# Loading the first four expert tiles on a condition of their own, in a conv, attention and mixture-of-experts kernel

## The chip, the cores and the metric

The kernel runs on one core of a Trainium2 chip. Time is the device time of one execution, in microseconds, as the median of several runs. The profile is of one further execution, which has its own time.

## The reference, cut to what matters

The input is 16 images of 256 channels and 14 by 14 points, all in float32. A bottleneck block of three convolutions with batch norms comes first, then linear attention over the 196 points of each image (a token is a point, 3136 in all), then a mixture of experts over all tokens:

```python
t = t + attention(layernorm(t))
flat = layernorm(t)                        # 3136 tokens x 256
probs = softmax(flat @ gate_w + gate_b)    # 8 experts
top_p, top_i = top_k(probs, 2)
top_w = top_p / (sum(top_p) + 1e-9)
for e in range(8):
    h = gelu(flat @ w1[e] + b1[e])         # 256 -> 1024
    y = h @ w2[e] + b2[e]                  # 1024 -> 256
    out += comb[:, e] * y                  # comb holds top_w at top_i, else 0
```

Every token goes to two experts, so the experts together get 6272 rows. The kernel computes an expert only on the rows that chose it.

## The kernel before, in words

**Three stretches.** First the convolutions. Then the attention as a software pipeline over the 16 images, in 25 slots (`SLOTS_A`), with the experts' weights split and stored beside it. Then the experts, as 56 slots (`SLOTS`) of one tile of 128 rows each, in the order of the experts.

**From the router to the experts.** Two images make a group, and there are 8 groups. For each group VectorE finds the two experts of each token (`route_top`), counts, and TensorE ranks the rows within their expert (`route_rank`); VectorE turns the ranks into row numbers (`route_slots`). GpSimd (POOL) then sends the rows to DRAM, to a buffer `norm_rows` (in the rows of the profile `rows_by_expert`) in which each expert has a region of 26 blocks of 128 rows: 8 indirect DMAs of 98 rows per group (`send_rows`, L440), which count on four semaphores `s_rows[g % 4]`, 128 for a group. A row is 265 numbers: 256 normalised values, 8 weights, and the token's number.

**The end of each expert.** The last tile of an expert is seldom full. So, once the counts are known, a block of 128 neutral rows (`padrow`) is written behind the last row of each expert (`pad_ends`, L260 to L265): experts 0 to 3 from the queue of SyncE (SP), 4 to 7 from that of ScalarE (ACT). Each pad is a register load of its address (L264) and a DMA (L265). One more pad, for the block that stands for "no tile", is written near the start of the kernel.

**The tile table.** TensorE sums the counts over the partitions (L812), and VectorE makes the table in 25 small dependent steps, counted by `s_tab` (`tile_table`, L1208 to L1278): for each slot the expert (`tbi[:, 0]`) and the block of `norm_rows` (`tbi[:, 1]`, "the column"), then packed forms of the experts, the end of each expert's run of tiles (`last_tile`), and a mask of experts by slot. The steps are a generator, and so interleaved with the last group's `route_slots`.

**The start of the experts.** ACT's stream at that place is: its four pads; a wait for the whole table; waits for all rows of all groups and for all pads; then `load_rows(0)`, `(1)`, `(2)`; then a loop of slots. Slot `m` of ACT holds, in this order, the copies of tile m-2's turned hidden values (L636), the copy of tile m's turned rows (L625), the gelu of tile m-1 (L630), and `load_rows(m + 3)`. One `load_rows` reads the block's number from the table into a register (L616) and issues a DMA of 128 rows (L619). TensorE waits for the table and then for tile 0's rows, transposes them (L829), and so on: transposes of a tile, then the first product of the tile before (L836), then the second product of the tile before that. VectorE adds biases (L1356, L1362), makes the low halves of the split operands (L1335, L1341), and scales; POOL adds the results to the output. SP, after its pads, reloads weights for experts 2 to 7, each when the last tile of the expert two before has passed.

Of the kernel before, what the change touches and what calls it, by code (L numbers as in the profile page):

```python
# [24 lines left out]
I32 = mybir.dt.int32  # L25
FR = mybir.dt.float32r
U32 = mybir.dt.uint32
ALU = mybir.AluOpType
# [45 lines left out]
RING = 8  # L74
XR, YS = 8, 4


# [6 lines left out]
def moe_block(nc, x, w1t, w2t, w3t, norms, res_scale, wqkv, wout, bout, gate_w, gate_b, ew1, ew2, eb, out):  # L84
# [5 lines left out]
    with ctx:  # L90
# [44 lines left out]

        cnti = sb("cnti", [128, E], I32)
        ntl = sb("ntl", [128, 2, E])
        lt = sb("lt", [128, E, E])
# [35 lines left out]
        with ExitStack() as scope:  # L174
            def mem(name, shape):
                return scope.enter_context(nc.sbuf_tensor(name, shape, F32))
            rows = mem("rows", [HALF, RING, 2, ROW])
            tc = mem("tc", [128, 2, 2, HW])
            xh = mem("xh", [HALF, 2, 2, C])
            qe = mem("qe", [HALF, 2, 2 * C])  # L180
            qn = mem("qn", [HALF, 2, 2 * C])
            ek = mem("ek", [128, 2, 2, HW])
            vT = mem("vT", [128, 3, 2, HW])
            ekt = mem("ekt", [HALF, 2, 2, C])
            cT = mem("cT", [128, 2, 2, 128])
            pr = mem("pr", [128, 2, 2, C])
            xT2 = mem("xT2", [128, 2, 2, HW])
        xr = sb("xr", [128, XR, ROW])
        xrTh = sb("xrTh", [128, 2, C], FR)
# [29 lines left out]
        s_tok = sem("token_numbers_written")  # L219
        s_ends = [sem(f"expert_ends_padded_by_{n}") for n in ("sync", "act")]  # L220
        s_res = sem("residual_written")
# [36 lines left out]


        def pad_ends(eng, which):  # L260

            eng.wait_ge(s_tab, 1)
            for e in range(which * E // 2, (which + 1) * E // 2):
                at = eng.value_load(pad_at[0:1, e:e + 1], min_val=0, max_val=128 * (NONE - 1))  # L264
                eng.dma_start(norm_rows[bass.ds(at, 128), :], padrow[:, :]).then_inc(s_ends[which], 16)  # L265


        @block.sync
        def _(sp):
# [58 lines left out]
            sp.wait_ge(s_const, NCONST)  # L328
            sp.dma_start(norm_rows[128 * NONE:128 * (NONE + 1), :], padrow[:, :]).then_inc(s_padw, 16)
            sp.dma_start(out[TOKENS:TOKENS + 128, :], padrow[:, 0:C]).then_inc(s_padw, 16)  # L330
# [8 lines left out]
            for n in range(SLOTS_A):  # L339
# [11 lines left out]
                if n == UNITS - EARLY + 2:  # L351
                    load_expert(1)
            pad_ends(sp, 0)
            sp.wait_ge(s_tab, TAB_STEPS)
# [6 lines left out]
        def _(pool):  # L361
# [92 lines left out]
            pool.wait_ge(s_res, 16 * B)  # L454
            pool.wait_ge(s_padw, 32)

# [15 lines left out]
        def _(act):  # L472
# [130 lines left out]

            act.activation(rs[:, 2:3], rs[:, 1:2], ACT.Gelu)
            pad_ends(act, 1)
            act.wait_ge(s_tab, TAB_STEPS)
            for a in range(RING // 2):
                act.wait_ge(s_rows[a], 128 * len(range(a, B // 2, RING // 2)))
            act.wait_ge(s_padw, 32)
            for a in range(2):  # L610
                act.wait_ge(s_ends[a], 16 * E // 2)
            blocks = norm_rows.rearrange("(c p) r -> c p r", p=128)

            def load_rows(i, r):
# [42 lines left out]
        def _(pe):  # L657
# [245 lines left out]
        def _(dve):  # L903
# [304 lines left out]
            def tile_table():  # L1208
                dve.wait_ge(s_cntp, 1)
                link(V.tensor_tensor(pad_at[:, :], psV[0:HALF, 0:E], expert_row[:, 0, :], ALU.add))  # L1210
                link(V.tensor_scalar(cnti[:, :], psV[:, 0:E], 127.0, None, ALU.add))
                yield
                dve.wait_ge(s_tab, tab[0])
                link(V.tensor_scalar(cnti[:, :], cnti[:, :], 7, None, ALU.logical_shift_right))
                yield
                dve.wait_ge(s_tab, tab[0])
                link(V.tensor_scalar(ntl[:, 0, :], cnti[:, :], 1.0, None, ALU.max))
# [8 lines left out]
                link(V.tensor_copy(last_tile[:, :], ntl[:, 1, :]))  # L1226
                yield
                dve.wait_ge(s_tab, tab[0])

                link(V.tensor_tensor(big[:, 0], iotf[:, 0:64].unsqueeze(2).to_broadcast([128, 64, E]),  # L1230
                                     ntl[:, 1, :].unsqueeze(1).to_broadcast([128, 64, E]), ALU.is_ge))
# [3 lines left out]
                yield  # L1235
                dve.wait_ge(s_tab, tab[0])
                link(V.tensor_tensor(big[:, 1], big[:, 0], ntl[:, 0, :].unsqueeze(1).to_broadcast([128, 64, E]), ALU.mult))
                yield
                dve.wait_ge(s_tab, tab[0])
                link(V.tensor_reduce(tb[:, 2, :], big[:, 1], X, ALU.add))  # L1240
                yield
                dve.wait_ge(s_tab, tab[0])
                link(V.tensor_tensor(tb[:, 3, :], iotf[:, 0:64], tb[:, 2, :], ALU.subtract))
                yield
                dve.wait_ge(s_tab, tab[0])
                link(V.scalar_tensor_tensor(out=tb[:, 3, :], in0=tb[:, 1, :], scalar=float(COLS), in1=tb[:, 3, :],
                                            op0=ALU.mult, op1=ALU.add))
                yield
                dve.wait_ge(s_tab, tab[0])
                link(V.tensor_scalar(tbi[:, 1, :], tb[:, 3, :], float(NONE), None, ALU.min))  # L1250
                yield
# [4 lines left out]
                link(V.tensor_copy(tbi[:, 0, :], tb[:, 4, :]))  # L1256
                yield
                dve.wait_ge(s_tab, tab[0])

                link(V.tensor_copy(tb[:, 0, 2:SLOTS + 2], tb[:, 4, 0:SLOTS]))  # L1260
# [152 lines left out]
MAGIC = 0x5F3759DF + 1  # L1413
TAB_STEPS = 25

# [43 lines left out]
```

## Time and profile before

| what | us |
|---|---|
| time, median of 3 runs | 719.97 (719.64 to 721.72) |
| the profiled execution, its own time | 723.74 |
| its span | 722.0 |
| TensorE busy in the span | 608.7 (84%) |
| VectorE busy | 461.9 (64%) |
| ScalarE busy | 317.4 (44%) |
| GpSimd busy | 211.7 (29%) |
| mean granted clock of TensorE | 0.928 of full speed |

The profiled execution's time is 1.74 us more than its span and 3.77 us more than the median. Starts are in microseconds from the start of the span. Busy shares are averages over the three stretches; what a change at one place is worth has to be read there.

### The profile page before, as it was taken

What the parts mean: (1) busy time and instruction counts of PE and PEld (TensorE: products, weight loads), DVE (VectorE), ACT (ScalarE), POOL (GpSimd) and SP (SyncE); (2) the same over time, 40 slices, a digit from 0 to 9 for tenths busy, and PEclk for the clock granted to TensorE, in tenths of its full rate; (3) what the DMA queues carried; (4) which work ended last, traced back from release to release, by engine and by line L of the source; (5) the groups of instructions that cost most, each with busy time, mean ns of one, the idle gap of its engine ahead of it and who ended that gap; (6) DMA issues with size and microseconds to landing.
All of it is one profiled execution on the core that took longest, in us unless ns stands there. A gap on an engine that the chain in (4) does not pass through costs nothing.

```text
span 722.0 us, 13716 instructions
## 1 busy us (share of the span) xinstructions
PE 608.7 (84%) x3882; PEld 539.0 (75%) x3882; DVE 461.9 (64%) x1491; ACT 317.4 (44%) x625; POOL 211.7 (29%) x193
## 2 busy tenths in 40 slices
PE   6663589889889985318999999999999999999991
PEld 3552477777777974317999899999999999999881
DVE  1788799898989776514556556556656656655641
ACT  1634577868676642103334334334343343343330
POOL 5230121212746556640212212212122122212211
PEclk9876699999999997559999999999999999999996
DMA  9490787868886972331237283552825627422211
GB/s 273 137 333 17 293 319 277 311 247 308 288 321 217 367 273 86 102 105 23 39 67 279 46 269 85 178 174 38 305 49 154 192 46 240 106 45 38 32 22 15
DMA packets 50516, 121.22 MB, mean 168 GB/s; under 512 B 7564, under 2 KB 39184, under 8 KB 44304
## 3 DMA queue, kind: packets, MB, share of 16 engines
q1 hardware_dynamic: 30128, 98.07, 37.5%
q0 software_dynamic: 11136, 14.00, 11.5%
q10 hardware_dynamic: 9184, 8.28, 4.1%
q8 instruction: 38, 0.62, 0.3%
q14 instruction: 30, 0.25, 0.1%
HBM read 68.22 MB, written 52.11 MB: 167 GB/s over the span
## 4 chain that ended last, share of the span: by engine, by line
PE 63%; DVE 21%; issue 6%; ACT 5%; ACTq 1%; DMA 1%; DVEq 0%; POOL 0%; another core or an unknown queue 0%; SPq 0%; POOLq 0%
PE ps L836 43%; PE ps L863 6%; DVE wset L1100 4%; PE ps L674 2%; DVE stt L1011 2%; PE ps L664 2%; PE ps L829 2%; PE ps L731 2%; ACT xh L535 1%; DVE img L1094 1%; PE ps L768 1%; DVE tc L1002 1%; ACT rows L535 1%; DVE bst L981 1%; ACT img L529 1%
## 5 line engine op out<-in xcount | busy, mean ns | idle before, releaser
L462 POOL DMA_INDIRECT out<-ys,xr x56 | 86.7, 1548 | 308.9 <-DVE ys L1367 235.2
L836 PE MATMUL ps<-wset,hTh 128*128 x896 | 161.7, 281 | 3.4 <-DVE hTl L1335 3.3
L836 PEld LDWEIGHTS ps<-wset,hTh 128*128 128x128 f32 x896 | 140.3, 188 | 10.6 <-issue 6.3
L836 PE MATMUL ps<-wset,xrTh 128*128 x448 | 147.4, 410 | 0.0
L630 ACT ACTIVATE hb<-hb 128x512 f32<-128x512 f32 x112 | 70.3, 632 | 135.4 <-DVE hb L1356 135.4
L836 PE MATMUL ps<-wset,hTl 128*128 x448 | 125.6, 280 | 0.0
L636 ACT CAST hTh<-ps 128x512 fp32r<-128x512 f32 x112 | 60.2, 590 | 99.1 <-PE ps L863 98.6
L1362 DVE TENSOR_TENSOR yb<-ps,bset 128x256 f32<-128x256 f32 x56 | 23.8, 425 | 123.9 <-PE ps L836 123.9
L836 PEld LDWEIGHTS ps<-wset,xrTh 128*128 128x128 f32 x448 | 81.2, 191 | 15.5
L836 PE MATMUL ps<-wset,xrTl 128*128 x224 | 89.5, 399 | 0.0
L1356 DVE TENSOR_TENSOR hb<-ps,bset 128x512 f32<-128x512 f32 x112 | 75.5, 685 | 18.1 <-PE ps L836 17.8
L836 PEld LDWEIGHTS ps<-wset,hTl 128*128 128x128 f32 x448 | 84.3, 188 | 0.0
L1335 DVE TENSOR_TENSOR hTl<-ps,hTh 128x512 fp32r<-128x512 f32 x112 | 71.8, 683 | 11.5 <-ACT hTh L636 8.2
L440 POOL DMA_INDIRECT rows_by_expert<-rows,slot x64 | 66.6, 1041 | 30.4 <-issue 22.0
L731 PE MATMUL ps<-xT,wq 128*128 128x196 f32 x256 | 51.5, 346 | 11.2 <-ACT vT L557 9.0
L416 POOL TENSOR_TENSOR img<-img,bo 98x512 f32<-98x512 f32 x16 | 20.4, 1275 | 133.9 <-ACT xh L535 130.2
L863 PE MATMUL ps<-ident,hb 128*128 128x128 f32 x448 | 58.2, 272 | 1.1 <-ACT hb L630 1.1
L731 PEld LDWEIGHTS ps<-xT,wq 128*128 128x128 f32 x256 | 45.1, 199 | 16.7 <-ACT xT L552 15.0
L863 PEld LDWEIGHTS ps<-ident,hb 128*128 128x128 f32 x448 | 50.3, 141 | 1.6 <-ACT hb L630 1.4
L836 PEld LDWEIGHTS ps<-wset,xrTl 128*128 128x128 f32 x224 | 42.8, 191 | 10.5
L829 PE MATMUL ps<-ident,xr 128*128 128x128 f32 x112 | 21.9, 278 | 21.4 <-DMA xr<-rows_by_expert 20.4
L1011 DVE BATCH_NORM_STATS2 stt<-img 98x6 f32<-98x256 f32 x64 | 25.0, 417 | 18.4 <-ACT img L529 18.0
(178 smaller groups left out, 946.7 us busy)
## 6 DMA issues: line engine op xcount, KB each, us to landing
split_weights<-wset SPq DMA_DIRECT2D x16, 2048.0 KB
wset<-split_weights SPq DMA_DIRECT2D x32, 1024.0 KB
wset<-in_ew SPq DMA_DIRECT2D x16, 1024.0 KB
xr<-rows_by_expert ACTq DMA_DIRECT2D x56, 132.5 KB, 2.2
bset<-in_eb SPq DMA_DIRECT2D x8, 640.0 KB
img<-in_x SPq DMA_DIRECT2D x8, 392.0 KB, 6.6
out<-img SPq DMA_DIRECT2D x16, 196.0 KB
rows_by_expert<-rows,slot POOLq DMA_INDIRECT x64
```

Source lines behind the costliest of these rows:

```text
L440: pool.indirect_dma_start(norm_rows, bass.IndirectOffsetOnAxis(slot[:, g % 2, k, t:t + 1], 0), rows[:, at, h, :], None).then_inc(s_rows[g ...
L462: pool.indirect_dma_start(out, bass.IndirectOffsetOnAxis(xr[:, r % XR, C + E:ROW].bitcast(U32), 0), ys[:, r % YS, :], None, compute_op=ALU ...
L630: act.activation(hb[:, p, h * 512:(h + 1) * 512], hb[:, p, h * 512:(h + 1) * 512], ACT.Gelu).then_inc(s_ge, 1)
L636: act.copy(hTh[:, p, h * 512:(h + 1) * 512], ps[:, 3 + h, :]).then_inc(s_hhi, 1)
L731: last = pe.matmul(dst[:, h * HW:(h + 1) * HW], wq[:, k, off + h * 128:off + (h + 1) * 128], xT[:, p, k, :], start=(k == 0), stop=(k == 1))
L829: last = pe.transpose(ps[:, 0, k * 128:(k + 1) * 128], xr[:, b, k * 128:(k + 1) * 128], ident[:, :])
L836: last = pe.matmul(dst, rows_k[:, k * 128:(k + 1) * 128], wset[:, bass.ds(column(k) + rest, width)], start=(k == 0 and n == 0), stop=(k == ...
L863: last = pe.transpose(ps[:, 3 + h, k * 128:(k + 1) * 128], hb[:, p, h * 512 + k * 128:h * 512 + (k + 1) * 128], ident[:, :])
L1011: V.bn_stats(stt[:, which, p, j, :], img[0:HALF, i, j * C:(j + 1) * C]).then_inc(S[stage]["vec"], 1)
L1100: V.tensor_tensor(part_lo[a], raw[a], part_hi[a].bitcast(F32), ALU.subtract).then_inc(s_lo_vec, 1)
L1335: V.tensor_tensor(hTl[:, p, part], ps[:, 3 + h, :], hTh[:, p, part].bitcast(F32), ALU.subtract).then_inc(s_hlo, 1)
L1356: V.tensor_tensor(hb[:, p, h * 512:(h + 1) * 512], ps[:, 1 + h, :], bset[:, bass.ds(off + h * 512, 512)], ALU.add).then_inc(s_hb, 1)
```

## The change

The first four tiles (`SOON`) no longer wait for everything. TensorE sums a second set of counts, that of the first seven groups, and VectorE works out for each of the four slots whether its tile is filled by those groups alone. The result is a flag of 0 or 1, turned into two thresholds: `128 + 128 * flag` for the semaphore that groups 3 and 7 share, and `16 + 128 * flag` for the pads. `load_rows(i)` for i < 4 reads both into registers and waits on them; `load_rows(4)` waits for all rows and all pads. Before the loads ACT waits for the first 21 steps of the table (`TAB_ROWS`) in place of all of them, for the semaphores of groups 0 to 6, and for group 3.

The table's steps are put in another order, so that the column of each tile comes after 21 steps, and the experts, `last_tile` and the packed forms after it; there are 34 steps now. The pads of all eight experts are issued by SP, one after another, and none by ACT. The buffer `rows` moves behind the other buffers of its scope, since the space at the front is used again for the loaded tiles.

```diff
+SOON = 4
@@ memory
-            rows = mem("rows", [HALF, RING, 2, ROW])
             tc = mem("tc", [128, 2, 2, HW])
...
             xT2 = mem("xT2", [128, 2, 2, HW])
+            rows = mem("rows", [HALF, RING, 2, ROW])
@@ SP
-        def pad_ends(eng, which):
-            eng.wait_ge(s_tab, 1)
-            for e in range(which * E // 2, (which + 1) * E // 2):
-                at = eng.value_load(pad_at[0:1, e:e + 1], min_val=0, max_val=128 * (NONE - 1))
-                eng.dma_start(norm_rows[bass.ds(at, 128), :], padrow[:, :]).then_inc(s_ends[which], 16)
...
-            sp.dma_start(norm_rows[128 * NONE:128 * (NONE + 1), :], padrow[:, :]).then_inc(s_padw, 16)
+            sp.dma_start(norm_rows[128 * NONE:128 * (NONE + 1), :], padrow[:, :]).then_inc(s_ends, 16)
...
-            pad_ends(sp, 0)
+            sp.wait_ge(s_ends, 16)
+            sp.wait_ge(s_tab, 1)
+            for e in range(E):
+                at = sp.value_load(pad_at[0:1, e:e + 1], min_val=0, max_val=128 * (NONE - 1))
+                sp.dma_start(norm_rows[bass.ds(at, 128), :], padrow[:, :]).then_inc(s_ends, 16)
             sp.wait_ge(s_tab, TAB_STEPS)
@@ ACT
-            pad_ends(act, 1)
-            act.wait_ge(s_tab, TAB_STEPS)
-            for a in range(RING // 2):
+            act.wait_ge(s_tab, TAB_ROWS)
+            for a in range(RING // 2 - 1):
                 act.wait_ge(s_rows[a], 128 * len(range(a, B // 2, RING // 2)))
-            act.wait_ge(s_padw, 32)
-            for a in range(2):
-                act.wait_ge(s_ends[a], 16 * E // 2)
+            act.wait_ge(s_padw, 16)
...
                 column = act.value_load(tbi[0:1, 1, bass.ds(i, 1)], min_val=0, max_val=NONE)
+                if i < SOON:
+                    last, ends = (act.value_load(latei[0:1, k, i:i + 1], min_val=m, max_val=16 * E + m)
+                                  for k, m in enumerate((128, 16)))
+                    act.wait_ge(s_rows[RING // 2 - 1], last)
+                    act.wait_ge(s_ends, ends)
+                if i == SOON:
+                    act.wait_ge(s_rows[RING // 2 - 1], 256)
+                    act.wait_ge(s_ends, 16 + 16 * E)
@@ TensorE
+                    pe.matmul(psV[:, E:2 * E], ones[:, :], run[:, (B // 2 + 1) % 2, :], start=True, stop=True)
                     pe.matmul(psV[:, 0:E], ones[:, :], run[:, (B // 2) % 2, :], start=True, stop=True).then_inc(s_cntp, 1)
@@ VectorE, tile_table: the steps added
+                link(V.tensor_scalar(cnti[:, 1, :], psV[:, E:2 * E], 0.0, None, ALU.add))
...
+                link(V.tensor_copy(ntl[:, 2, :], cnti[:, 1, :]))
...
+                link(V.tensor_scalar(ntl[:, 3, :], ntl[:, 0, :], -1.0, float(COLS), ALU.mult, ALU.add))
+                link(V.tensor_tensor(ntl[:, 4, :], ntl[:, 2, :], ntl[:, 0, :], ALU.subtract))
...
+                link(V.tensor_tensor(ntl[:, 5, :], ntl[:, 1, :], ntl[:, 4, :], ALU.add))
...
+                link(V.tensor_tensor(whole[:, :, :], iotf[:, 0:SOON].unsqueeze(2).to_broadcast([128, SOON, E]),
+                                     ntl[:, 5, :].unsqueeze(1).to_broadcast([128, SOON, E]), ALU.is_ge))
...
+                link(V.tensor_tensor(whole[:, :, :], whole[:, :, :], big[:, 0, 0:SOON, :], ALU.subtract))
...
+                link(V.tensor_reduce(late[:, :], whole[:, :, :], X, ALU.add))
...
+                link(V.tensor_scalar(latei[:, 0, :], late[:, :], 128.0, 128.0, ALU.mult, ALU.add))
+                link(V.tensor_scalar(latei[:, 1, :], late[:, :], 16.0 * E, 16.0, ALU.mult, ALU.add))
+                assert tab[0] == TAB_ROWS, tab[0]
@@ the two counts
-TAB_STEPS = 25
+TAB_ROWS = 21
+TAB_STEPS = 34
```

## Rows read from the trace of the kernel before

**Rows 1.** The page, part 2: busy tenths of PE in 40 slices of the span.

```profile
PE   6663589889889985318999999999999999999991
```

**Rows 2.** Busy time by stretch: us, each engine's busy (instructions), granted clock, DMA share, GB/s.

```profile
300.00:320.00 20.00, 0.81 (x5) 0.68 (x5) 7.61 (x29) 0.00 (x0) 12.66 (x14) 0.50 0.41 128
320.00:328.00 8.00, 5.74 (x15) 4.42 (x16) 1.77 (x5) 1.37 (x3) 0.00 (x0) 0.50 0.25 66
...
360.00:690.00 330.00, 329.92 (x2255) 302.04 (x2254) 191.66 (x440) 127.61 (x245) 75.59 (x49) 1.00 0.47 128
```

**Rows 3.** The chain that ended last, in order of time: start, us, what.

```profile
309.30 8.63 issue
...
318.22 0.28 ACTq L616
...
318.88 2.16 DMA xr<-rows_by_expert
...
321.87 0.38 ACT xrTh L625
...
323.58 5.02 PE ps L836 x12
```

**Rows 4.** The timeline of POOL: the last sending of group 6 and of group 7.

```profile
304.77 0.96 POOL L440 DMA_INDIRECT rows_by_expert<-rows,slot  x1 [0.30 <-issue]
...
315.36 0.96 POOL L440 DMA_INDIRECT rows_by_expert<-rows,slot  x1 [0.31 <-issue]
```

**Rows 5.** L608, the waits of ACT for the rows: ns min/median/max, then the start.

```profile
L608 ACTq EVENT_SEMAPHORE  x1: 17/17/17, 317.9 to 317.9; - x1
```

**Rows 6.** The timeline of DVE, table steps: start, us.

```profile
301.03 0.16 DVE L1211 TENSOR_SCALAR cnti<-ps 128x8 int32<-128x8 f32 x1
...
305.89 0.20 DVE L1250 TENSOR_SCALAR tbi<-tb 128x64 int32<-128x64 f32 x1
...
308.47 0.69 DVE L1277 TENSOR_TENSOR big<-tb,iotf 128x512 f32<-128x512 f32 x1
```

**Rows 7.** L616 and L619, the parts of a load_rows: ns min/median/max, first and last start.

```profile
L616 ACTq TENSOR_LOAD <-tbi x56: 275/280/594, 318.2 to 672.9; - x56
L616 ACTq FUSED_REGOPS  x56: 152/152/158, 318.5 to 673.2; - x56
...
L619 ACTq MOVE xr<-rows_by_expert x56: 29/29/38, 318.8 to 673.5; - x56
```

**Rows 8.** L264, address loads of the pads, in 300 to 304: ns min/median/max.

```profile
L264 ACTq TENSOR_LOAD <-pad_at x3: 420/458/490, 301.1 to 303.7; - x3
L264 ACTq FUSED_REGOPS  x2: 162/164/167, 301.7 to 303.0; - x2
```

**Rows 9.** L265, the pads, over the whole span.

```profile
L265 ACTq DMA_DIRECT2D rows_by_expert<-padrow x4: 13/384/690, 302.1 to 308.6; - x4
L265 SPq MOVE rows_by_expert<-padrow x4: 3/14/695, 302.9 to 314.9; - x4
L265 SPq DMA_DIRECT2D rows_by_expert<-padrow x4: 6/10/707, 302.9 to 316.3; - x4
```

**Rows 10.** DMA of 315 to 316 us, SP's queue: packets, MB, share of 16 engines.

```profile
q1 hardware_dynamic: 144, 0.14, 39.6%
```

**Rows 11.** The timeline of ACT in the first slots, with tile 4's load.

```profile
330.14 0.34 ACTq L619 DMA_DIRECT2D xr<-rows_by_expert  x1
```

**Rows 12.** The timelines of DVE and of SP: tile 0's bias, the end of expert 0.

```profile
328.74 0.69 DVE L1356 TENSOR_TENSOR hb<-ps,bset 128x512 f32<-128x512 f32 x1 [1.64 <-PE ps L836]
...
376.23 10.05 SPq L322 DMA_DIRECT2D wset<-split_weights  x4
```

**Rows 13.** L812, the sum of the counts on PE.

```profile
L812 PE MATMUL ps<-run,ones x2: 362/372/383, 298.5 to 298.7; 98*128 98x8 f32 x2
```

**Rows 14.** The waits of PE in 290 to 330: us in total, times, longest.

```profile
PE ps L829 <- DMA xr<-rows_by_expert: 20.4, 1, 20.4
```

More of the change, by code:

```diff
@@ L134, in moe_block @@
         pad_at = sb("pad_at", [HALF, E], I32)
-        cnti = sb("cnti", [128, E], I32)
-        ntl = sb("ntl", [128, 2, E])
+        cnti = sb("cnti", [128, 2, E], I32)
+        ntl = sb("ntl", [128, 6, E])
+        whole = sb("whole", [128, SOON, E])
+        late = sb("late", [128, SOON])
+        latei = sb("latei", [128, 2, SOON], I32)
         lt = sb("lt", [128, E, E])
@@ L219, in moe_block @@
         s_tok = sem("token_numbers_written")
-        s_ends = [sem(f"expert_ends_padded_by_{n}") for n in ("sync", "act")]
+        s_ends = sem("expert_ends_padded")
         s_res = sem("residual_written")
@@ L454, in _ @@
             pool.wait_ge(s_res, 16 * B)
-            pool.wait_ge(s_padw, 32)
+            pool.wait_ge(s_padw, 16)
             def add_rows(i, r):
@@ L1210, in tile_table @@
                 link(V.tensor_tensor(pad_at[:, :], psV[0:HALF, 0:E], expert_row[:, 0, :], ALU.add))
-                link(V.tensor_scalar(cnti[:, :], psV[:, 0:E], 127.0, None, ALU.add))
+                link(V.tensor_scalar(cnti[:, 0, :], psV[:, 0:E], 127.0, None, ALU.add))
+                link(V.tensor_scalar(cnti[:, 1, :], psV[:, E:2 * E], 0.0, None, ALU.add))
                 yield
                 dve.wait_ge(s_tab, tab[0])
-                link(V.tensor_scalar(cnti[:, :], cnti[:, :], 7, None, ALU.logical_shift_right))
+                link(V.tensor_scalar(cnti[:, :, :], cnti[:, :, :], 7, None, ALU.logical_shift_right))
                 yield
                 dve.wait_ge(s_tab, tab[0])
-                link(V.tensor_scalar(ntl[:, 0, :], cnti[:, :], 1.0, None, ALU.max))
+                link(V.tensor_scalar(ntl[:, 0, :], cnti[:, 0, :], 1.0, None, ALU.max))
+                link(V.tensor_copy(ntl[:, 2, :], cnti[:, 1, :]))
                 yield
@@ L1225, in tile_table @@
                 dve.wait_ge(s_tab, tab[0])
-                link(V.tensor_copy(last_tile[:, :], ntl[:, 1, :]))
+                link(V.tensor_tensor(big[:, 0], iotf[:, 0:64].unsqueeze(2).to_broadcast([128, 64, E]),
+                                     ntl[:, 1, :].unsqueeze(1).to_broadcast([128, 64, E]), ALU.is_ge))
+                link(V.tensor_tensor(ntl[:, 5, :], ntl[:, 1, :], ntl[:, 4, :], ALU.add))
                 yield
                 dve.wait_ge(s_tab, tab[0])
-                link(V.tensor_tensor(big[:, 0], iotf[:, 0:64].unsqueeze(2).to_broadcast([128, 64, E]),
-                                     ntl[:, 1, :].unsqueeze(1).to_broadcast([128, 64, E]), ALU.is_ge))
+                link(V.tensor_tensor(big[:, 1], big[:, 0], ntl[:, 3, :].unsqueeze(1).to_broadcast([128, 64, E]), ALU.mult))
+                link(V.tensor_tensor(whole[:, :, :], iotf[:, 0:SOON].unsqueeze(2).to_broadcast([128, SOON, E]),
+                                     ntl[:, 5, :].unsqueeze(1).to_broadcast([128, SOON, E]), ALU.is_ge))
+                yield
+                dve.wait_ge(s_tab, tab[0])
+                link(V.tensor_reduce(tb[:, 2, :], big[:, 1], X, ALU.add))
+                link(V.tensor_tensor(whole[:, :, :], whole[:, :, :], big[:, 0, 0:SOON, :], ALU.subtract))
+                yield
+                dve.wait_ge(s_tab, tab[0])
+                link(V.tensor_tensor(tb[:, 3, :], iotf[:, 0:64], tb[:, 2, :], ALU.add))
+                link(V.tensor_reduce(late[:, :], whole[:, :, :], X, ALU.add))
+                yield
+                dve.wait_ge(s_tab, tab[0])
+                link(V.tensor_scalar(tbi[:, 1, :], tb[:, 3, :], float(NONE), None, ALU.min))
+                link(V.tensor_scalar(latei[:, 0, :], late[:, :], 128.0, 128.0, ALU.mult, ALU.add))
+                link(V.tensor_scalar(latei[:, 1, :], late[:, :], 16.0 * E, 16.0, ALU.mult, ALU.add))
+                assert tab[0] == TAB_ROWS, tab[0]
                 yield
@@ L1234, in tile_table @@
                 link(V.tensor_reduce(tb[:, 1, :], big[:, 0], X, ALU.add))
[L1235 to L1250, printed above, removed]
+                link(V.tensor_copy(last_tile[:, :], ntl[:, 1, :]))
                 yield
@@ L1256, in tile_table @@
                 link(V.tensor_copy(tbi[:, 0, :], tb[:, 4, :]))
-                yield
-                dve.wait_ge(s_tab, tab[0])
                 link(V.tensor_copy(tb[:, 0, 2:SLOTS + 2], tb[:, 4, 0:SLOTS]))
```

## The prediction, made before the changed kernel was run

> **What bounds the kernel now.** I read the page first, for where TensorE is not busy. It is the bound of the expert stretch: a digit of 9 in nearly every slice [rows 1], and 329.92 of the 330 us between 360 and 690 [rows 2], in which POOL adds 49 tiles, so 6.73 us a tile. The hole is in slices 17 and 18. By stretch, TensorE works 0.81 us in the 20 us from 300 to 320, and then starts at a granted clock of 0.50, the level of 1.2 GHz, before it has 1.00, 2.4 GHz [rows 2]. Since the expert stretch is a train of tiles with TensorE full, whatever brings its start forward brings the end forward by as much, and the only question is when tile 0 and its followers can go.
>
> The chain in order of time says what the hole waits for: 8.63 us of nothing on ACT from 309.30, then the register load of tile 0's block at 318.22, its DMA at 318.88, which takes 2.16 us, and the copy of its turned rows on ACT at 321.87 [rows 3]. ACT was in its waits for the rows (L608) until 317.9 [rows 5]. What it waited for is POOL's last indirect DMA, started at 315.36 [rows 4]: 2.57 us from its start to the release. POOL is the slow one there: the last sending of group 6 and that of group 7 are 8 sendings and 10.59 us apart, 1.32 us each. So before, tile 0 waits for rows that mostly belong to other tiles.
>
> **The change part by part.**
>
> *The release of tile 0.* Group 6's last sending starts at 304.77 [rows 4]; with the same 2.57 us its rows have landed at 307.3. The table must have its columns by then. Before, they are there at 306.1, 5.1 us after the first step at 301.03 [rows 6]. Three dependent steps go from ahead of them (the copy to `last_tile`, the first big reduce, the multiply-add), about 0.2, 0.7 and 0.25 us at the pitch of these steps, and nine small ones come in beside others, which I take at 0.1 us each, since they start in the shadow of an independent neighbour. The second sum of counts on TensorE puts two more passes of 0.37 us, partly overlapped, before the table starts [rows 13], say 0.4 us. Sum: 306.1 - 1.2 + 0.9 + 0.4 = 306.2, still 1.1 us under the rows. The whole table, which TensorE still waits for before tile 0, ends at 309.2 before [rows 6] and near 309.8 after; tile 0's rows come later than that (below), so this costs nothing. If the table were as late as 307.3, each further microsecond would count in full.
>
> *The three loads ahead of tile 0.* In ACT's order all of `load_rows(0)` to `(2)` come ahead of tile 0's copy. A register load costs 0.28 + 0.15 us [rows 7] and some 0.1 us for a check and the gaps, 0.54 us in all; from 318.22 to 318.88 is such a load and what little stands ahead of the DMA's issue [rows 3], which takes 0.38 us [rows 9], so a whole `load_rows` is about 1.05 us. Now each has three register loads, and two waits of some 0.07 us. In the quiet this adds 1.2 us to each. But these loads now run while POOL's rows are in flight, and the register loads done in that state, the ones for the pads, took 0.46 us, not 0.28, with 0.16 behind them [rows 8], so 0.72 each. I take that row, as the nearer one: 3 x 0.72 + 0.14 + 0.5 for the DMA's issue is 2.8 us per tile, 8.4 for three. ACT needs 0.28 us from its release to its first load (317.94 to 318.22 [rows 3, 5]). So: 307.3 + 0.3 + 8.4 = 316.0, and the copy of tile 0's turned rows starts there, where it was 321.87. Tile 0's own rows have long landed: issued at 310.4, landed 2.2 us later, turned by 313.4. **The gain is 5.8 us.** By the quiet price it is 7.4.
>
> The Trainium skill (DMA: Bandwidth & Descriptors, Latency and other measured facts) gives a register load from a tensor a floor of about 600 ns. By that, an estimate, nine loads would cost 0.14 us each more than I charge and the gain would be 4.5 us; the trace has 0.28 us [rows 7], so the measured ones stand.
>
> *Behind tile 0.* `load_rows(3)` follows tile 0's copy and is 1.7 us longer than before, so tile 1's copy is that much later; it is wanted only for tile 1's product, a whole slot on, and costs nothing. `load_rows(4)` has no new register loads but the full wait. ACT came to it at about 330.0 [rows 11], 8.1 us after tile 0's copy, so it comes to it at 324.1 now. Behind this wait on ACT stand the copies of tile 0's turned hidden values (L636), for which VectorE and TensorE wait at once; a late pad stops the whole train. Group 7's rows are no matter: they land at 317.9, since POOL's pace is untouched.
>
> *The pads on one queue.* ACT's four pads go away (they were over by 309.3, under the wait for rows, so this gains nothing by itself) and SP has eight. At ACT's first pace, some 1.3 us a pad (0.46 + 0.16 + 0.38 for the DMA, and the gaps [rows 8, 9]), SP would issue the last at 303.4 + 7 x 1.3 = 312.5 and it would land near 314.7, 9 us ahead of the need at 324.1. They cost nothing while a pad takes under (321.9 - 303.4)/7 = 2.6 us. Up to 3.5 us the gain shrinks; beyond it the kernel is slower. Before, the pads took 2.2 us each on ACT and 4.5 on SP [rows 9], which is where the danger is (rivals).
>
> *The rest.* SP's later weight loads depend on tiles and move with them. The buffer `rows` at another address and one wait fewer on POOL change no duration. The flags: expert 0 ends at tile 7, for SP is released to reload its weights at 376.2, 46.8 us or seven tile times after tile 0's bias [rows 12]. Eight tiles are over 896 rows; seven of eight groups would hold near 780 of these, and four whole tiles need 512. So all four flags should be 0.
>
> The profiled execution would be 723.74 - 5.8 = 717.9; with the same 3.77 us to the median, **714.2 us**.
>
> **Rivals.**
>
> *A: the pads are late, slower.* From about 304 to 318, SP's and ACT's instructions run at some 0.7 us each, even a plain register MOVE (up to 695 ns, where 29 is normal) [rows 7, 9]. SP went on so when ACT had no pads left, and took 13.4 us for the three steps between its four pads. If this pace holds for all eight, the last is issued at 303.4 + 7 x 4.46 = 334.6, lands at 336.6, and ACT passes tile 4's wait 6.5 us later than the 330.1 of before: 726.5 us. For it: it is the only row of SP alone with pads. Against it: the records look delayed themselves. The shortest MOVE is 3 ns, and the packets of SP's last pad move between 315 and 316, before its recorded issue at 316.3 [rows 9, 10]. A stall in writing records would be absent from an untimed-by-profile run, which is what the median is. The Trainium skill says that the block that writes trace records can push back on the engines (NOTIFIC — the notification-queue block, section 7.1, overflow); no run here shows whether it does.
>
> *B: ACT is slowed too, no gain.* If ACT's instructions also take 0.7 us until the rows have all landed at 317.9, the 14 instructions of `load_rows(0)` take 9.8 us, to 317.4; the other two go at 2.2 us each, and tile 0's copy is at 321.8: the time of before, 720.
>
> *C: half of A.* SP's slow pace ends at 318 with the last rows, as it did before. Then SP has issued four pads by 316.3, as before, and the other four at 1 to 1.3 us each by 323; the last lands at 325, and the train stands for 1 us at tile 4. Gain 5, time 715.
>
> *D: a flag is 1.* Then tile 0 waits as before, and pays for the longer loads and the single queue: 721 to 724. The rows speak against it.
>
> **How the numbers follow.** Forecast as worked out 0.64, C 0.07, B 0.14, A 0.14, D 0.01. The forecast's own range is 711 to 717: the quiet price of the loads gives 712.6; rows of group 6 landing 1 us later beside the pads give 715.2; and tile 0's first product ran for 5.02 us at the lower clock [rows 3], half of which can come or go with the place where the clock rises, 2.5 us to either side. To hold 8 in 10 the range goes on to B: 711 to 720.5. What this kernel's measurement can tell from no change is 0.3%, 2.2 us. Faster by more: forecast and C, 0.71; within it: B, 0.15; slower: A and most of D, 0.14.
>
> **What the profile after would show.** Right: L619's first DMA near 310, the first three 2.8 us apart, tile 0's copy (L625) near 316; the idle of TensorE before L829 down from 20.4 us [rows 14] to about 12; ACT not idle at tile 4's load. SP's eight pads in 11 us confirm the cheap queue; eight in over 20 us, with ACT's hidden copies (L636) of tile 0 waiting, is A. A first DMA at 317 or later is B, or D if the wait stands on the shared semaphore. If the profiled execution shows slow pads and the untimed runs are fast all the same, the slow instructions belong to the recording. The prediction is wrong in its size if the register loads are quick, or if the granted clock rises at another place than in tile 0's first product.

## The result, and the profile after

The changed kernel takes 714.82 us (714.61 to 715.06, 4 runs), beside 720.44 us for the kernel before on the same chip. The ratio is 0.9917, interval 0.9902 to 0.9932: 5 to 7 us faster. Forecast were 714.2 us and a gain of 5.8 us.

The profiled execution has 714.77 us and a span of 713.0, so it stands at the median. The one of before that the prediction was made from does not: it has 3.8 us more than its median, and part of that lies ahead of the experts. Group 7's last sending starts at 315.36 there [rows 4] and at 312.23 in a later profile of the same kernel (below). So starts in the two profiles must not be subtracted as they are; I measure from a landmark inside each, the start of group 6's last sending.

Part 2 of the page after, TensorE's busy tenths, to be held against [rows 1]:

```profile
PE   6653579888889996439999999999999999999991
```

The digits of slices 16 to 19 were 5, 3, 1, 8 and are 6, 4, 3, 9: the hole is shorter. The waits of TensorE from 290 to 330 say what is left (columns as in [rows 14]):

```profile
PE ps L837 <- DMA xr<-rows_by_expert: 12.6, 1, 12.6
...
PE ps L837 <- DVE xrTl L1352: 2.2, 1, 2.2
```

12.6 us of waiting for tile 0's rows, where it was 20.4. The second line is new: tile 1's transposes now wait for tile 0's low half, 2.2 us after 1.1 before.

The sendings of POOL in the timeline after, to be held against [rows 4]: the last of group 6, and the last of group 7.

```profile
302.88 0.96 POOL L441 DMA_INDIRECT rows_by_expert<-rows,slot  x1 [0.30 <-issue]
...
313.17 0.95 POOL L441 DMA_INDIRECT rows_by_expert<-rows,slot  x1 [0.30 <-issue]
```

And ACT, its waits and loads by line (ns min/median/max, first and last start), and two lines of its timeline:

```profile
L608 ACTq EVENT_SEMAPHORE  x1: 38/38/38, 305.9 to 305.9; - x1
L615 ACTq TENSOR_LOAD <-tbi x4: 279/378/582, 306.1 to 313.6; - x4
L617 ACTq TENSOR_LOAD <-latei x8: 272/304/479, 306.9 to 314.7; - x8
L623 ACTq EVENT_SEMAPHORE  x1: 17/17/17, 321.3 to 321.3; - x1
...
308.40 5.19 ACTq L626 DMA_DIRECT2D xr<-rows_by_expert  x3
313.63 0.37 ACT L632 CAST xrTh<-ps 128x256 fp32r<-128x256 f32 x1 [18.22 <-DMA rows_by_expert<-rows,slot]
```

ACT is let go at 305.9, while POOL has six of group 7's eight sendings still to start. The three loads follow one another until 313.6, and tile 0's copy (L632) starts the moment they are over. TensorE had tile 0 turned before that, so ACT's own stream holds the copy:

```profile
311.82 0.66 PE L837 MATMUL ps<-ident,xr 128*128 128x128 f32 x2 [12.62 <-DMA xr<-rows_by_expert]
```

The wait for all rows and pads, ahead of tile 4's load, is passed at 321.3 (L623) without a stop: SP's pads are long out.

```profile
L354 SPq MOVE rows_by_expert<-padrow x8: 29/29/38, 300.5 to 308.4; - x8
L354 SPq DMA_DIRECT2D rows_by_expert<-padrow x8: 332/332/383, 300.6 to 308.5; - x8
```

Eight pads in 7.9 us, 1.13 us each, and no MOVE above 38 ns. The table, in DVE's timeline: the columns, the last threshold, and the end of the table.

```profile
303.86 0.23 DVE L1257 TENSOR_SCALAR tbi<-tb 128x64 int32<-128x64 f32 x1
...
304.08 0.16 DVE L1259 TENSOR_SCALAR latei<-late 128x4 int32<-128x4 f32 x1
...
307.13 0.69 DVE L1288 TENSOR_TENSOR big<-tb,iotf 128x512 f32<-128x512 f32 x1
```

It is ready at 304.24, 1.7 us ahead of the release.

### The profile page after: what moved, and what is told of

It is laid out like the page before. It is cut to its first block, busy times and chain, and to the rows that moved or that the text cites. A ratio compares the mean times of both kernels' runs of the same rounds, so it can differ in the third digit from the quotient of the medians.

```text
span 713.0 us, 13755 instructions
## 1 busy us (share of the span) xinstructions
PE 609.1 (85%) x3884; PEld 539.4 (76%) x3884; DVE 461.8 (65%) x1500; ACT 317.6 (45%) x625; POOL 211.6 (30%) x193
## 4 chain that ended last, share of the span: by engine, by line
PE 64%; DVE 21%; issue 5%; ACT 5%; POOL 2%; DMA 1%; DVEq 0%; SPq 0%; ACTq 0%; POOLq 0%
PE ps L844 44%; PE ps L871 6%; DVE wset L1108 4%; DVE stt L1019 2%; PE ps L671 2%; PE ps L738 2%; PE ps L837 2%; PE ps L775 2%; POOL rows_by_expert L441 2%; PE ps L727 2%; PE ps L681 1%; DVE tc L1010 1%; ACT xh L536 1%; DVE img L1102 1%; DVE bst L989 1%
## 5 line engine op out<-in xcount | busy, mean ns | idle before, releaser
L1346 DVE TENSOR_TENSOR hTl<-ps,hTh 128x512 fp32r<-128x512 f32 x112 | 71.8, 683 | 11.2 <-ACT hTh L643 7.8
L738 PE MATMUL ps<-xT,wq 128*128 128x196 f32 x256 | 51.0, 344 | 11.2 <-ACT vT L558 9.5
L417 POOL TENSOR_TENSOR img<-img,bo 98x512 f32<-98x512 f32 x16 | 20.4, 1273 | 134.5 <-ACT xh L536 134.5
L844 PEld LDWEIGHTS ps<-wset,xrTl 128*128 128x128 f32 x224 | 42.7, 190 | 10.3
L837 PE MATMUL ps<-ident,xr 128*128 128x128 f32 x112 | 21.9, 278 | 14.8 <-DMA xr<-rows_by_expert 12.6
```

Of the source, the lines that this page charges most:

```text
L738: last = pe.matmul(dst[:, h * HW:(h + 1) * HW], wq[:, k, off + h * 128:off + (h + 1) * 128], xT[:, p, k, :], start=(k == 0), stop=(k == 1))
L837: last = pe.transpose(ps[:, 0, k * 128:(k + 1) * 128], xr[:, b, k * 128:(k + 1) * 128], ident[:, :])
L844: last = pe.matmul(dst, rows_k[:, k * 128:(k + 1) * 128], wset[:, bass.ds(column(k) + rest, width)], start=(k == 0 and n == 0), stop=(k == ...
L1346: V.tensor_tensor(hTl[:, p, part], ps[:, 3 + h, :], hTh[:, p, part].bitcast(F32), ALU.subtract).then_inc(s_hlo, 1)
```

## The experiments

The theory: the gain is the condition of tile 0, it is the difference between POOL's sendings of groups 6 and 7 less what ACT's three longer loads take, and neither the pads' queue nor the table's order pays by itself. The main rivals: one queue for the pads is what pays (the profile of before had slow instructions with pads on two), or what stands behind tile 4's load is not urgent. Every run but the profiles of before is timed against the kernel before on its own chip.

### The pads on one queue, alone

The kernel before, with one line moved:

```diff
             pad_ends(sp, 0)
+            pad_ends(sp, 1)
...
-            pad_ends(act, 1)
```

> The kernel before, with the pads of all eight experts on SP's queue and no other part of the change. Theory (the gain is tile 0's earlier condition): tile 0 still waits for POOL's last rows, which land at the same moment, so 720.4 us, within 1 us, unless eight pads on SP take over 14 us; with the 4.5 us a pad of the profile of before it would be 30 us and the time 735. Rival (the gain is from pads leaving ACT, and from one queue): most of the 5.6 us is here, 715 to 716. In the profile: eight pads in 8 to 10 us, none with a register instruction of 0.7 us, if the slow instructions of before come from two queues with pads at once.

Measured: 720.57 us, ratio 0.9998 (0.9979 to 1.0016). The single queue is worth nothing by itself. The pads took 8.0 us, none slow. The lines by line, SP's pads and ACT's wait for the rows:

```profile
L265 SPq DMA_DIRECT2D rows_by_expert<-padrow x8: 332/332/381, 298.6 to 306.6; - x8
...
L608 ACTq EVENT_SEMAPHORE  x1: 17/17/17, 314.3 to 314.3; - x1
```

The last pad is issued 7.7 us before ACT is let go, by POOL's rows. The 4.5 us a pad of the first profile, which would have made 735, are not there.

### The condition, with the pads on two queues

The changed kernel, with experts 4 to 7 padded by ACT ahead of its waits:

```diff
-            for e in range(E):
+            for e in range(E // 2):
                 at = sp.value_load(...); sp.dma_start(...)
...
+            act.wait_ge(s_ends, 16)
+            act.wait_ge(s_tab, 1)
+            for e in range(E // 2, E):
+                at = act.value_load(...); act.dma_start(...)
             act.wait_ge(s_tab, TAB_ROWS)
```

> The changed kernel, with the pads of experts 4 to 7 put back on ACT, ahead of its waits. Theory: ACT has four pads to issue before its first load, 5 us from 299.5 at its quick pace and so over before group 6's rows land at 305.9: 714.8, within 1 us, if instructions stay quick. Rival: with pads on both queues the instructions of SP and ACT go at 0.7 us each as in the profile of before; ACT's 14 instructions of tile 0's load then take up to 9.8 us and the gain is gone: 718 to 721. Which of the two in the timed runs, and whether the profile shows slow instructions, also tells whether the slowness belongs to the recording.

Measured: 715.36 us, ratio 0.9922 (0.9901 to 0.9943), the changed kernel's within the intervals. ACT's pads by line, the release, and the last sending of group 6:

```profile
L610 ACTq MOVE rows_by_expert<-padrow x4: 29/29/37, 299.0 to 302.5; - x4
...
L613 ACTq EVENT_SEMAPHORE  x1: 38/38/38, 306.5 to 306.5; - x1
...
300.91 1.09 POOL L441 DMA_INDIRECT rows_by_expert<-rows,slot  x1 [0.30 <-issue]
```

ACT's instructions are quick and its pads are over at 303.0. Yet it is let go only at 306.5, 5.6 us after group 6's last sending began; with one queue it was 3.0. So the rows landed later where both queues moved pads beside them, an effect that neither theory had. The pads themselves took longer too: 3.4 and 4.2 us from issue to landing in the median of the two queues, for 2.6 on one [after, L354]. To see what it is worth, three kernels ran on one chip: this one, the changed one and the best one (below).

> The changed kernel again, on one chip with the two runs after this, so that the three can be set against each other. 714 to 715.5 us, ratio near 0.992. In its profile tile 0's copy comes 10.5 to 11 us after the start of group 6's last sending, the release 3.0 after it. If the first profile's late start of the sendings (302.88 where the other versions have 300.4 to 301.7) was chance of that chip, it is near 301 here, and the time up to 1.5 us lower.

> The changed kernel with the pads on two queues again. In its first profile the pads of both queues moved within 5 us, and group 6's last rows landed 5.6 us after their sending began, where it is 3.0 with one queue; tile 0's copy came 12.95 us after it, for 10.75. If that is the rule, the single queue is worth 1 to 2 us once tile 0 waits for group 6, and this is slower than the changed kernel on the same chip by that. If it was chance, the two are even.

The changed kernel: 713.87 us, ratio 0.9905 (0.9887 to 0.9923). With two queues: 714.36 us, 0.9923 (0.9902 to 0.9944). By profile the late landing is there again: 5.8 us here, 2.7 in the changed kernel.

```profile
L613 ACTq EVENT_SEMAPHORE  x1: 38/38/38, 305.0 to 305.0; - x1
...
299.22 1.09 POOL L441 DMA_INDIRECT rows_by_expert<-rows,slot  x1 [0.30 <-issue]
```

From that sending's start to tile 0's copy it is 12.96 us with two queues (12.95 in the first run) and 10.78 with one (10.75). The times do not show these 2.2 us: 0.5 us lies between the medians, inside the intervals. The profiles say where they are masked: the changed kernel is late ahead of the experts. Its group 6 is sent last at 302.9 and 302.8 in its two profiles, where these two have 300.9 and 299.2; it is so on both chips, so chance of one chip, which the first expectation above considered, is not the reason. Most of it can be found. From 233 to 237 us, in the attention, TensorE's granted clock fell to 1.2 GHz in both profiles of the changed kernel, and stayed at 2.4 GHz there in every other profile but the slow one (0.638, below). By stretch, first the changed kernel and then this one, and one product (L727, here L732) of each:

```profile
233.00:237.00 4.00, 3.85 (x14) 3.09 (x15) 3.36 (x17) 3.18 (x7) 0.64 (x1) 0.59 1.01 304
233.00:237.00 4.00, 4.00 (x25) 3.45 (x26) 3.18 (x15) 3.36 (x8) 0.46 (x1) 1.00 0.99 339
...
234.48 3.20 PE L727 MATMUL ps<-wq,xT 128*98 128x256 f32 x8
233.94 1.89 PE L732 MATMUL ps<-wq,xT 128*98 128x256 f32 x8
```

From the start of the product ahead of this one to the start of the one behind it, it is 4.37 us in the changed kernel and 2.69 here, 1.7 us more. TensorE had the same work and the same waits (0.3 and 0.7 us) ahead of them in both, so why the clock fell in both profiles of the changed kernel and in no other stays open. What is shown is that rows land 2.6 to 3.1 us sooner with the single queue, and that tile 0's copy then comes 2.2 us sooner after group 6's last sending; what the queue is worth in time is not shown.

### Everything but the condition

```diff
-                    last, ends = (act.value_load(latei[0:1, k, i:i + 1], min_val=m, max_val=16 * E + m)
-                                  for k, m in enumerate((128, 16)))
-                    act.wait_ge(s_rows[RING // 2 - 1], last)
-                    act.wait_ge(s_ends, ends)
+                    act.wait_ge(s_rows[RING // 2 - 1], 256)
+                    act.wait_ge(s_ends, 16 + 16 * E)
```

> The changed kernel, with everything but the condition: the first four loads wait for all rows and all pads, and read no flag. Theory: 720.4, within 1 us. If the table's new order, the memory order or the single queue had a share in the gain, the time is between 715 and 719.

Measured: 719.04 us, ratio 0.9978 (0.9964 to 0.9992). I expected nothing, and 1.5 us is there, with an interval of 0.6 to 2.6. The profile shows where about half of it is. In this kernel the wait for group 7 stands behind the register load of tile 0's block; before, it stood ahead of it. The line of the load and that of the DMAs:

```profile
L615 ACTq TENSOR_LOAD <-tbi x6: 277/282/687, 303.7 to 328.6; - x6
...
L624 ACTq DMA_DIRECT2D xr<-rows_by_expert x6: 345/349/372, 313.5 to 329.3; - x6
```

The load starts at 303.7, ten microseconds ahead of the DMA. POOL's last sending starts at 310.84 in this profile, and tile 0's DMA follows it by 2.7 us; it is 3.5 us in the first profile of before [rows 3, 4] and in its third (below; the second was slow). So 0.8 us is the register load out of the way. Another 0.5 us is POOL's: from group 6's last sending to group 7's it is 10.44 us here, and 10.9 in the third profile of before and in that with the pads moved alone. Tile 0's first product also ran shorter, 4.24 us for 5.02 before [rows 3], but from tile 0's copy to the end of the span it is 400.1 us here, and 400.1 and 400.5 in the same two profiles of before, so this brought the end at most some tenths.

```profile
318.27 4.24 PE ps L842 x12
```

None of this is a share of the changed kernel's gain. There the last wait is that for group 6, and the load of tile 0's block stands behind it (released at 305.9, load at 306.1), as it stood behind the last wait before.

### Constants in place of the registers

The first four loads wait for what the flags would say, as if known:

```diff
-                    last, ends = (act.value_load(...) for k, m in enumerate((128, 16)))
-                    act.wait_ge(s_rows[RING // 2 - 1], last)
-                    act.wait_ge(s_ends, ends)
+                    act.wait_ge(s_rows[RING // 2 - 1], 128)
+                    act.wait_ge(s_ends, 16)
```

This kernel is right only where expert 0 fills four tiles with the first seven groups' rows, as here.

> The changed kernel, where the first four loads wait for the constants 128 and 16 in place of two registers, as if all four flags were known to be 0. Theory: ACT's stream is what sets tile 0 now (its copy waits 1.1 us behind load 2), and each load loses two register loads, 1.2 us: tile 0's DMA goes out at 306.8 in place of 308.4 and its copy comes at 310.5 in place of 313.6, then bound by its own rows; 714.8 - 3 = 711.7. Rival (ACT's order does not matter, the rows in flight set it): 714 to 715.

Measured: 711.09 us, ratio 0.9861 (0.9844 to 0.9877), 0.4 to 0.6% under the changed kernel's two ratios; 711.7 was expected. From ACT's timeline and PE's:

```profile
309.04 0.37 ACT L630 CAST xrTh<-ps 128x256 fp32r<-128x256 f32 x1 [15.88 <-PE ps L835]
...
308.34 0.66 PE L835 MATMUL ps<-ident,xr 128*128 128x128 f32 x2 [11.39 <-DMA xr<-rows_by_expert]
```

The copy comes right behind the transposes now, and 8.4 us after group 6's last sending (300.62), where the changed kernel has 10.75. So the register loads for flags do cost 2.3 us at tile 0's copy, and with them gone tile 0's own rows set the start. The times differ by 3 to 4 us, but this is not all the flags: 1.7 us of it is the lower clock from 233 to 237, which the profiles of the changed kernel have and this one has not. These are slower than in the quiet: DMA at 304.8, transposes at 308.3, and 3.4 us from issue to landing beside pads and POOL's rows, for 2.2 before.

### The pads late

Only tiles 4 and on depend on the pads. The changed kernel, with SP held back:

```diff
             sp.wait_ge(s_ends, 16)
+            sp.wait_ge(s_hb, 1)
             sp.wait_ge(s_tab, 1)
```

> The changed kernel, where SP holds its eight pads back until tile 0's first bias is added, 318.9 in the profile after. Theory: tiles 0 to 3 need no pad and start as before this edit; tile 4's wait, which ACT reaches at 321.3, holds ACT until the last pad lands, near 318.9 + 1.2 + 7 x 1.15 + 2.1 = 330.2, with tile 0's hidden copies queued behind it: 8.9 us later, 714.8 + 8.9 = 723.7, the slower case that was priced as a rival. Rival (nothing urgent stands behind tile 4's load, its rows have 9 us to spare): 715 to 716.

Measured: 724.02 us, ratio 1.0043 (1.0027 to 1.0059), so slower than before, and 1.3% over the changed kernel's first ratio: 9.1 us, where 8.9 were expected. By line and in ACT's timeline: the last pad at 326.1, the wait for the pads passed at 328.0, the copy of tile 0's hidden values.

```profile
L355 SPq DMA_DIRECT2D rows_by_expert<-padrow x8: 332/332/380, 318.4 to 326.1; - x8
...
L624 ACTq EVENT_SEMAPHORE  x1: 17/17/17, 328.0 to 328.0; - x1
...
328.58 1.07 ACT L644 CAST hTh<-ps 128x512 fp32r<-128x512 f32 x2 [8.19 <-DMA rows_by_expert<-padrow]
```

ACT stood 8.19 us, and the first four tiles' early start was lost and more. The forecast was hit partly by luck. Counted from group 6's last sending, the wait for the pads is passed 7.9 us later than in the changed kernel (26.3 us for 18.4). Then TensorE, idle from 324.1 to 330.7, fell to 1.2 GHz at 329 and stayed there until 335.8, so what follows tile 0's hidden copy takes 3.1 us more; and this kernel's sendings come 1.2 us earlier. Of the change's hazards this is the large one, and the single queue of pads has 10 us of room against it.

### One flag, read ahead of the rows

The reduce over experts becomes one over tiles and experts, a maximum, and ACT reads the two thresholds once, ahead of all waits for rows, which move behind the first column's load:

```diff
-                link(V.tensor_reduce(late[:, :], whole[:, :, :], X, ALU.add))
+                link(V.tensor_reduce(late[:, :], whole[:, :, :].rearrange("p a e -> p (a e)"), X, ALU.max))
...
             act.wait_ge(s_tab, TAB_ROWS)
+            last, ends = (act.value_load(latei[0:1, k, 0:1], ...) for k, m in enumerate((128, 16)))
-            (the waits for s_rows[0..2] and s_padw)
...
                 column = act.value_load(...)
+                if i == 0:
+                    (the waits for s_rows[0..2] and s_padw)
+                    act.wait_ge(s_rows[RING // 2 - 1], last)
+                    act.wait_ge(s_ends, ends)
```

> The changed kernel with one flag for the first four tiles in place of four, read once and ahead of the waits for rows, with the first column. Six of eight register loads for flags go, and what is left lies in the shadow of the rows. Theory: as quick as the run with constants, 711.1, or up to 0.7 us quicker, since its first column is now loaded before the release: 710.4 to 711.1. Rival (the register loads now delay the release, as the table is ready only 1.7 us ahead of the rows): 712 to 713.

Measured: 709.91 us, ratio 0.9866 (0.9828 to 0.9904), the best median of all; by ratio it is even with the constants. It ran once more on the chip of the changed kernel's second run:

> The version with one flag again. 709.5 to 711 us, 4 to 5 us under the changed kernel on the same chip, as the loads in line ahead of tile 0's copy are two register loads per tile fewer and the rest lies ahead of the rows.

710.83 us there, 0.9867 (0.9844 to 0.9890), 3.0 us under the changed kernel's median, somewhat less than expected. By profile tile 0's copy comes 2.8 us sooner after group 6's last sending (7.94 for 10.78). It holds for any input, since a flag of 1 makes tile 0 wait as before. The thresholds' loads, the wait for the first three semaphores, and the first DMA, by line, in the first of the two profiles:

```profile
L607 ACTq TENSOR_LOAD <-latei x2: 287/423/559, 302.1 to 303.0; - x2
...
L618 ACTq EVENT_SEMAPHORE  x1: 17/17/17, 304.1 to 304.1; - x1
...
L626 ACTq DMA_DIRECT2D xr<-rows_by_expert x7: 339/345/367, 304.5 to 329.7; - x7
```

The table is ready at 302.1, and 2.4 us of register loads and issue later the DMA goes out: ACT passes its waits for the rows at 304.1, 0.2 us behind its last register load, so the rows have stopped being what it waits for.

### The flag from six groups

The running counts get a third buffer, the second set is summed after group 5, and ACT waits for groups 0 to 5 alone:

```diff
-        run = sb("run", [HALF, 2, E])
+        run = sb("run", [HALF, 3, E])
...
-  ... run[:, (B // 2 + 1) % 2, :]
+  ... run[:, (B // 2 - 2) % 3, :]
...
-                    for a in range(RING // 2 - 1):
+                    for a in range(RING // 2 - 2):
...
+                    act.wait_ge(s_rows[RING // 2 - 2], last)
...
                 if i == SOON:
+                    act.wait_ge(s_rows[RING // 2 - 2], 256)
```

> The run before this with the flag worked out from the first six groups, and ACT waiting for groups 0 to 5 alone (expert 0's rows in them fill five tiles). Theory: the rows are then landed before the table's columns are there at 304.2, so the table and three register loads set tile 0; they end near 306, where the rows of group 6 let go at 305.9, so nothing or up to 0.5 us is won over one flag: 710.2 to 711. Rival (the rows still set tile 0): 1.5 us or more is won.

Measured: 710.43 us, ratio 0.9874 (0.9844 to 0.9903): nothing on top of one flag, as forecast. The table is ready at 303.0 (L607's first load) and the DMA goes out at 305.3, 2.3 us later, the same as above.

```profile
L607 ACTq TENSOR_LOAD <-latei x2: 282/411/540, 303.0 to 303.8; - x2
...
L628 ACTq DMA_DIRECT2D xr<-rows_by_expert x7: 339/345/367, 305.3 to 330.6; - x7
```

### The kernel before, profiled again

> The kernel before, once more, for a second profile. If the register instructions of 0.7 us belong to two queues with pads in flight beside POOL's rows, they are here again; if they were chance of one execution, they are not, as in the run with two queues. The start of group 7's sending (306.23 in the first profile) should be 2 to 4 us earlier if the first profile's extra 3.8 us lay ahead of the router.

This execution ran at a mean granted clock of 0.638 and took 931.62 us; no time of it is used. Its register instructions were not slow: SP's MOVE 29/29/38 ns, eight pads on two queues in 4.1 us.

> The kernel before, for a third profile, since the second fell in an execution at a granted clock of 0.638. If the slow register instructions are chance, they are absent: MOVE at 29 ns, eight pads in about 5 us on two queues. Its own time should be within 719 to 722, and POOL's last sending near 311 to 312, as in the runs derived from it, in place of 315.36.

This execution took 720.92 us, at the median. By line, the pads of SP and of ACT, and in the timeline the last sending:

```profile
L265 ACTq DMA_DIRECT2D rows_by_expert<-padrow x4: 343/365/407, 298.9 to 302.3; - x4
L265 SPq MOVE rows_by_expert<-padrow x4: 29/29/38, 298.9 to 302.7; - x4
...
312.23 0.96 POOL L440 DMA_INDIRECT rows_by_expert<-rows,slot  x1 [0.30 <-issue]
```

Group 7's first sending starts at 302.87, 3.4 us earlier than in the first profile (306.23), so what that profile had too much lay ahead of the experts.

## Why the prediction was right

*The place and the release: right.* With everything but the condition the gain is 1.5 us, and by its profile 1.3 of it come from two things that do nothing for the changed kernel: the order of one register load, and POOL's pace in group 7. With the condition, and the pads left on two queues, all of the gain is there, within the intervals. The rows of group 6 landed 3.0 and 2.7 us after their last sending's start, for the 2.57 I took; pads were in flight beside them.

*The loads: right in kind, a little dear.* I charged 8.4 us for three; they took 7.5 us (306.1 to 313.6), and 8.0 in the second profile of the changed kernel. I took 0.46 us for a register load; they were 0.30 us in the median in the first and up to 0.58 [after, L615 and L617], 0.38 and up to 0.74 in the second. By the quiet price it would have been 6.8 us (8.4 less the 1.6 by which the gain grows then). The constants' run shows that this term is real: without the loads for flags tile 0's copy comes 2.3 us earlier.

*The sum: right at its place, and in part luck as a time.* The prediction took it that whatever brings the start of the tiles forward brings the end forward by as much. All profiles bear it out but that with the late pads, in which the train stands still behind its start. From the profiles, in microseconds:

| profile | group 6 sent last | to tile 0's copy | from there to the end | span |
|---|---|---|---|---|
| before, first | 304.77 | 17.10 | 400.1 | 722.0 |
| before, third | 301.30 | 17.43 | 400.5 | 719.2 |
| changed | 302.88 | 10.75 | 399.4 | 713.0 |
| changed, again | 302.81 | 10.78 | 399.2 | 712.8 |
| pads on one queue, alone | 300.84 | 17.59 | 400.4 | 718.8 |
| condition, two queues | 300.91 | 12.95 | 399.9 | 713.8 |
| the same, again | 299.22 | 12.96 | 400.1 | 712.3 |
| all but the condition | 300.40 | 16.17 | 400.1 | 716.7 |
| constants | 300.62 | 8.42 | 400.7 | 709.7 |
| late pads | 301.72 | 10.39 | 410.7 | 722.8 |
| one flag | 300.75 | 7.32 | 399.9 | 708.0 |
| one flag, again | 300.14 | 7.94 | 400.3 | 708.4 |
| six groups | 301.03 | 7.82 | 399.9 | 708.7 |

From group 6's last sending to tile 0's copy I had 17.1 us before [rows 3, 4] and 11.2 after, a gain of 5.8. Measured are 10.75 after, and 17.4 in the third profile of before, whose time is at the median: 6.7 us. The differences are the register loads (0.9 too dear), the landing (0.4 too cheap) and 0.3 us that the first profile of before was short. The timed gain is 5.6 us and, in the second comparison, 6.4, with intervals that reach from 5 to 8. That it lies so near 5.8 is in part chance, for two things that I left out nearly cancel. Against the third profile of before, the changed kernel gains 1.1 us more behind tile 0's copy (400.5 to 399.4; why is not shown), and loses 1.6 us ahead of the experts (301.30 to 302.88), about the 1.7 us of the lower clock from 233 to 237: 6.7 + 1.1 - 1.6 = 6.2 us, the difference of the two spans.

*The table: right.* I had its columns at 306.2 against a landing at 307.3, and its end near 309.8. Shifted by the 1.9 us that the profile after is earlier at group 6, that is 304.3 and 307.9; it shows 304.1 and 307.8.

*The pads: right, and the rival's mechanism too.* They cost nothing, at 1.13 us a pad, and 1.3 was assumed. That the choice of queue moves the landing of the rows beside them was no part of the prediction. That a late pad stops the whole train is shown by the run that made them late: 9.1 us, of which 7.9 are the longer wait.

*Rivals A, B and C did not occur.* They rested on instructions of 0.7 us in one profile [rows 9]. In the thirteen other profiles, with one queue or two, of the kernel before or of others, no MOVE of a pad is above 38 ns; only single register loads reach 0.6 to 0.76 us. What made all of them slow in that one execution is open. Recording may have a part (packets ahead of the issue's record, [rows 9, 10]), but no run here shows it.

*Rival D did not occur*: tile 0's DMA went out before group 7's last sendings.

## What to carry to other kernels

When a consumer waits for a producer's whole output, look at which part it needs first, and put the slow producer's tail under it; here eight indirect DMAs of 1.3 us each had only to come out of tile 0's condition. Then count what the finer condition itself issues on the waiting engine: reading thresholds tile by tile put tile 0's copy 2.3 us later than constants did, and one combined flag, read before the data can be there, put it no later than constants. A wait placed in an in-order stream must be priced by what stands behind it, not by the load that it guards, and a price from a single profile should be checked against a second before it is believed.

## What the runs showed of the hardware that was not expected

A register load from memory on ACT took 0.28 us in the quiet and up to 0.76 us while indirect DMAs and pads were in flight. The DMA of a tile's rows took 2.1 to 2.2 us from issue to landing in the quiet, and up to 3.4 beside pads and sendings in the changed kernel and in the run with constants, up to 4.0 in that with one flag. The rows of an indirect DMA landed 2.6 us after its start with no pad in flight (the pads moved alone, and the late pads), 2.7 to 3.2 with pads on one queue (four profiles), and 5.6 to 5.8 with the same pads on two queues at once (two profiles).

TensorE's first product after the hole, 12 matmuls in the chain, ran for 5.0 to 5.1 us in three profiles (the first and the third of before, and the one with the pads moved alone; TensorE idle ahead of tile 0 for 20.3 to 20.5 us), and for 4.1 to 4.7 us in nine others (10.3 to 18.6 us idle). By stretch, the granted clock after, from 313 to 320 and from 320 to 328, to be held against [rows 2]:

```profile
313.00:320.00 7.00, 5.32 (x17) 4.30 (x18) 1.77 (x5) 1.38 (x3) 0.95 (x1) 0.57 0.26 73
320.00:328.00 8.00, 6.88 (x48) 6.09 (x47) 3.84 (x8) 3.25 (x6) 0.00 (x0) 1.00 0.10 23
```

The product starts at the lower level, 1.2 GHz, in all twelve, and the clock is at 2.4 GHz before its end. After, this was at 319.0, 3.7 us behind the product's start (315.34); before, at 328.3, 4.7 us behind it (323.58), with the product's end at 328.6. The product itself is 0.3 to 1.1 us shorter in the nine, but little of that reaches the end: from tile 0's copy to the end of the span it is 399.2 to 400.7 us in the nine and 400.1 to 400.5 in the three. Why the clock rises earlier in the product was not tried.
